# Text rows of two batches first, a table piece ahead of two slots, a later table sum, and block 0's rows by matmuls

## The reference, cut to what matters

```
h = concat([patches @ proj_w.T + proj_b + pos, txt])
xn = layernorm(layernorm(h)) * ln_w
Q = xn[:, None] * W_qk ; attn = softmax(causal(Q @ Q.T / sqrt(192)))
h = h + ((attn @ (xn - mean(wte))) / (row + 1)) @ W_o.T       # wte: 50257 x 192
n = rmsnorm(layernorm(h)) * ffn_ln_w
probs = softmax(n @ w_router) ; expert = argmax(probs)         # 16 experts
keep  = rank of the token within its expert and batch <= 64
y = relu(n @ wi[expert]) @ wo[expert]   if kept, else n
h = h + layernorm(h) + max(probs) * y
```

## Time and profile before

| | |
|---|---|
| median of 3 runs | 367.31 us (365.68 to 370.08) |
| profiled execution | 367.87 us, span 366.0 us |
| TensorE busy | 334.5 us, 91% |
| Vector, Pool, Scalar busy | 228.0, 167.7, 126.2 us |
| mean granted clock of TensorE | 0.967 |
| Vector busy from 200 to 210 us | 9.83 of 10 us |
| share of the transfer engines, 20 to 60 us | 1.01 to 1.06 |
| idle of Scalar, waiting for row maxima | 51.2 us |

### The profile page before, as it was taken

The page is one execution under the profiler, slowest core; times in us unless marked ns, Lnnn a source line. Parts: engine busy times, 40 slices in busy tenths (PEclk is TensorE's granted clock), DMA queues, the critical chain, the costliest instruction groups (busy, mean ns, idle before and its releaser), DMA issues.

```text
span 366.0 us, 6697 instructions
## 1 busy us (share of the span) xinstructions
PE 334.5 (91%) x2336; PEld 306.0 (84%) x2336; DVE 228.0 (62%) x557; ACT 126.2 (34%) x437; POOL 167.7 (46%) x180
## 2 busy tenths in 40 slices
PE   8499969899999999999998979999949999999992
PEld 3388859799899898997997969999815999999991
DVE  0669768789688787796888977657485222222221
ACT  2056543552545436534545024446610111111110
POOL 3173943755854846657548011250661134444321
PEclk9969989999999999999999978999998999999997
DMA  8899999289999995799997969400232699999940
GB/s 252 264 430 282 260 247 217 77 170 230 219 232 230 196 239 143 139 236 270 246 211 199 324 191 289 112 2 1 100 107 73 183 293 266 266 264 260 266 118 17
DMA packets 21096, 74.29 MB, mean 203 GB/s; under 512 B 3540, under 2 KB 9173, under 8 KB 20306
## 3 DMA queue, kind: packets, MB, share of 16 engines
q1 hardware_dynamic: 11362, 43.16, 38.5%
q0 software_dynamic: 6800, 27.82, 37.0%
q10 hardware_dynamic: 2912, 3.04, 3.0%
HBM read 66.12 MB, written 9.25 MB: 206 GB/s over the span
## 4 chain that ended last, share of the span: by engine, by line
PE 66%; DVE 13%; DMA 8%; ACT 5%; issue 5%; ACTq 1%; POOL 0%; POOLq 0%; DVEq 0%
PE bO L1224 18%; PE bS L1224 15%; PE bE L1224 14%; PE bJ L1224 12%; DMA wx<-in_wte 6%; ACT PB L563 2%; DMA hB<-in_txtB 2%; PE bT L1311 2%; DVE wx L856 1%; PE bT L1576 1%; DVE wbuf L856 1%; PE bT L1317 1%; PE bT L1270 1%; DVE oTA L823 1%; ACT pay L620 1%
## 5 line engine op out<-in xcount | busy, mean ns | idle before, releaser
L423 POOL TENSOR_TENSOR PA<-PA,rn 128x512 f32<-128x512 f32 x24 | 25.4, 1057 | 81.5 <-DVE rn L813 81.5
L401 POOL TENSOR_TENSOR AwA<-zT,w 96x512 f32<-96x512 f32 x45 | 50.1, 1192 | 17.4 <-ACT zT L540 17.4
L1224 PE MATMUL bJ<-wo_sb,oTA 128*128 128x192 f32 x288 | 52.7, 333 | 0.0
L558 ACT ACTIVATE PA<-bS,negmax 128x128 f32<-128x128 f32 x96 | 34.0, 367 | 51.3 <-DVE negmax L801 51.2
L1224 PEld LDWEIGHTS bS<-zT,AwA 96*128 96x128 f32 x384 | 47.3, 194 | 1.3 <-issue 0.2
L1224 PEld LDWEIGHTS bJ<-wo_sb,oTA 128*128 128x128 f32 x288 | 47.4, 194 | 0.0
L1224 PE MATMUL bS<-zT,AwA 96*128 96x128 f32 x384 | 47.1, 276 | 0.0
L1224 PE MATMUL bO<-PA,wx 96*128 96x112 f32 x384 | 45.4, 275 | 0.5 <-DVE PA L1197 0.5
L1224 PEld LDWEIGHTS bO<-PA,wx 96*128 96x128 f32 x384 | 44.9, 192 | 0.7 <-DVE PA L1197 0.7
L468 POOL DMA_INDIRECT out<-PA,yrow x16 | 15.1, 942 | 56.0 <-DVE PA L1213 56.0
L695 ACT ACTIVATE AwA<-bO 128x448 f32<-128x448 f32 x16 | 8.7, 544 | 78.5 <-PE bO L1224 52.9
(11 more groups left out here) (252 smaller groups left out, 705.5 us busy)
## 6 DMA issues: line engine op xcount, KB each, us to landing
wbuf<-in_wte POOLq DMA_DIRECT2D x10, 1344.0 KB, 12.7
wx<-in_wte POOLq DMA_DIRECT2D x8, 1344.0 KB, 12.0
wx<-in_wi SPq DMA_DIRECT2D x16, 576.0 KB
wx<-in_wo SPq DMA_DIRECT2D x16, 576.0 KB
wx<-in_wte SPq DMA_DIRECT2D x12, 672.0 KB, 9.2
dispatched<-zeros SPq DMA_DIRECT2D x7, 675.5 KB, 9.0
wbuf<-in_wte SPq DMA_DIRECT2D x2, 1344.0 KB, 7.0
wx<-in_wte SPq DMA_DIRECT2D x2, 1344.0 KB, 17.6
```

The costliest lines, as they stand in the source:

```text
L401: nc.gpsimd.tensor_tensor(o, zT[:, k, ss].unsqueeze(1).to_broadcast(list(o.shape)), w2[:, k, hs].unsqueeze(2).to_broadcast(list(o.shape)), ...
L423: nc.gpsimd.tensor_tensor(t, t, q.unsqueeze(2).to_broadcast(list(t.shape)), ALU.mult).then_inc(p_ready, 1)
L558: last = nc.scalar.activation(PA[:, h, :], bank[:, j * SA:(j + 1) * SA], ACT.Exp, bias=negmax[:, h:h + 1], accum_out=lsum[:, h:h + 1])
L1224: return nc.tensor.matmul(o, l, r, start=start, stop=stop, skip_group_check=True)
```

## The change

- Text tails and text rows of batches 0 and 1 are loaded and summed ahead of the others, on both queues; the constants come behind the small loads. The squared weights are made first on Vector. factors(1, 2, 2) stands ahead of a wait, the variances of batches 2 to 7 ahead of batch 0's first low part. The router's scaled weights are made within batch 0. One matmul of ones at the start is dropped.
- Sync loads plain piece 0 behind wo_attn, ahead of slots 2 and 3, and waits for tok_ready 5 there. Pool adds one chunk in batch 0 and three in each of batches 1 to 5; before it was 2, 3, 3, 2, 3, 3. In batch 0 Vector does plain_sum 1 behind the second maximum.
- In batch 6 TensorE does the second scores before wte_mean. On Vector a row maximum and a low part stand inside table_total, and mean_rows and mean_text come behind e_copy, row_factor and value_low. Transpositions and projections alternate anew.
- Block 0's transposed rows are made by 22 matmuls of norm with a 0/1 matrix (select, dispatch): where a token's place equals the column's number. Sync loads block 1's rows first. Scalar waits for the scatters before it loads block 3's. The rows of tokens that were not kept are made around block 0. stay_warm goes from 3, 10 and 26 to 8 and 6.

```
+        SEL0, SEL1 = 2 * EMB + 2 * T, XBUF * DW + FC * T
+        sels = ((0, 6, paf[:, SEL0:SEL0 + 6 * T].rearrange("p (j c) -> p j c", j=6)),
+                (6, SLOTS, Awf[:, SEL1:SEL1 + (SLOTS - 6) * T].rearrange("p (j c) -> p j c", j=SLOTS - 6)))
         posI, dropI = sb("posI", [128, SLOTS], i32), sb("dropI", [128, SLOTS], i32)
...
-
-            for q in range(XBUF):
+        def for_blocks(eng, step):
+
+            step(0, 0)
+            nb = count_blocks(eng)
+            for q in range(1, XBUF):
                 step(0, q)
...
-            def plain_loads(sp):
-
-                sp.wait_ge(tok_ready, 5)
-                for n in range(WPLAIN):
+            def plain_loads(sp, n0, n1):
+
...
-                sp.dma_start(H[p0:p1, 0:NBATCH, :], txtA[p0 - IMG:p1 - IMG]).then_inc(txt_in, 16)
+            for b0, b1, arrived in ((0, 2, txt_in), (2, NBATCH, txt2_in)):
+                for p0, p1 in ((IMG, 116), (116, 128)):
+                    sp.dma_start(H[p0:p1, b0:b1, :], txtA[p0 - IMG:p1 - IMG, b0:b1]).then_inc(arrived, 16)
             sp.dma_start(H[0:BP, NBATCH:SLOTS, :], txtBp).then_inc(late_in, 16)
...
             sp.wait_ge(cst_in, 16)
-            sp.wait_ge(hb_in, 16)
+            sp.wait_ge(hb2_in, 16)
             sp.wait_ge(pos_in, 32)
             sp.wait_ge(w_in, 32)
-            sp.wait_ge(txt_in, 32)
+            sp.wait_ge(txt2_in, 32)
             for s in range(2):
                 sp.dma_start(wchunk[s], wv[:, s, :]).then_inc(wte_first[s], 16)
             sp.dma_start(wo_sb[:, :, :], wo_attn).then_inc(wo_in, 16)
+            sp.wait_ge(tok_ready, 5)
+            plain_loads(sp, 0, 1)
             for s in range(2, WBUF):
                 sp.dma_start(wchunk[s], wv[:, s, :]).then_inc(wte_first[s], 16)
             sp.dma_start(cst2[:], cst2_d[:, 0:C_MAT]).then_inc(cst2_in, 16)
             sp.dma_start(wtail[:], wte[VOCAB - WTAIL:VOCAB, :]).then_inc(wtail_in, 16)
-
-            plain_loads(sp)
+            plain_loads(sp, 1, WPLAIN)
...
-            for q in range(XBUF - 1):
+            for q in (1, 0, 2):
...
                 for c in chunks[0:1]:
-                    add_wte(c)
+                    if c is not None:
+                        add_wte(c)
...
-                iteration(b, range(WBUF + 2 + 16 * b // 6, WBUF + 2 + 16 * (b + 1) // 6))
+                c = WBUF + 3 * b
+                iteration(b, range(c, c + 3) if b else (None, WBUF + 2))
...
-            act.dma_start(cst[:], cst_d).then_inc(cst_in, 16)
+            act.dma_start(hB[:, 0:2, :], txtB[:, 0:2]).then_inc(hb_in, 16)
             for dst, src in ((w2[:], wqk), (ln96[:], lnw)):
                 act.dma_start(dst, src).then_inc(w_in, 16)
             for dst, src in ((posb, pos), (pbb, projb)):
                 act.dma_start(dst, src).then_inc(pos_in, 16)
-            act.dma_start(hB[:], txtB).then_inc(hb_in, 16)
+            act.dma_start(cst[:], cst_d).then_inc(cst_in, 16)
+            act.dma_start(hB[:, 2:NBATCH, :], txtB[:, 2:NBATCH]).then_inc(hb2_in, 16)
...
-                if h == 3:
+                if h == 7:
...
-            nt_copy(0)
             exps(LAST, (1,))
             o_copy(b, 3)
+            values(LAST)
+            nt_copy(0)
             nt_copy(1)
-            values(LAST)
+            exps(LAST, (2,))
             nt_copy(2)
             nt_copy(3)
...
-                if not (is0(i) and q == 0):
+                if is0(i) and q == 0:
+                    act.wait_ge(scattered, 16 * SLOTS)
+                else:
                     act.wait_ge(y_ready, b)
...
+            def text_stats(b0, b1):
+                for b in range(b0, b1):
+                    last = nc.vector.bn_stats(st6[0:SB, 1, b, :], hB[:, b, :])
+                link(last)
+                for b in range(b0, b1):
+                    last = nc.vector.bn_aggr(mv[0:SB, 1, b, :], st6[0:SB, 1, b, :])
+                link(last)
+
+            dve.wait_ge(w_in, 16 * 2)
+            link(nc.vector.tensor_tensor(w2[:, :, :], w2[:, :, :], ln96[:, :].unsqueeze(2).to_broadcast([EC, 2, HEADS]), ALU.mult))
+            link(nc.vector.tensor_tensor(w2[:, :, :], w2[:, :, :], w2[:, :, :], ALU.mult))
+            nc.vector.tensor_scalar(w2[:, :, :], w2[:, :, :], float(EMB) ** -0.5, None, ALU.mult).then_inc(w2_ready, 1)
...
+                row_max(LAST, 0)
                 link(nc.vector.tensor_tensor(chunk_rows(w, 0, 3), chunk_rows(w, 0, 3), chunk_rows(p, 0, 3), ALU.add))
                 link(nc.vector.tensor_tensor(chunk_rows(w, 0, 3), chunk_rows(w, 0, 3), chunk_rows(w, 3, 6), ALU.add))
+                t_low(LAST - 1, 3)
                 nc.vector.tensor_tensor(chunk_rows(w, 0, 1), chunk_rows(w, 0, 1), chunk_rows(w, 1, 2), ALU.add)
                 link(nc.vector.tensor_tensor(chunk_rows(w, 2, 3), chunk_rows(w, 2, 3), chunk_rows(w, 6, 7), ALU.add))
...
+            factors(1, 2, 2)
             dve.wait_ge(t_used, 1)
             nc.vector.tensor_tensor(AwB[:, 0, :, :], zT[:, 0, SA:SEQ].unsqueeze(1).to_broadcast([EC, HEADS, SB]),
                                     w2[:, 0, :].unsqueeze(2).to_broadcast([EC, HEADS, SB]), ALU.mult).then_inc(awB0_ready, 1)
-            factors(1, 2, 2)
+            dve.wait_ge(hb2_in, 16)
+            text_stats(2, NBATCH)
...
             dve.wait_ge(t_ready, 1)
             z(1)
             row_factor(0, 2)
+            variances(2, NBATCH)
             def b_rows(b):
...
                 e_copy(b, 0)
                 t_low(b, 2)
                 e_copy(b, 1)
+                if is0(b):
+                    dve.wait_ge(late_in, 16 * 5)
+                    nc.vector.memset(oneX[:], 1.0)
+                    nc.vector.tensor_tensor(wr_sb[:, :, :], wr_sb[:, :, :], flc[:, :].unsqueeze(2).to_broadcast([EC, 2, EXP]),
+                                            ALU.mult).then_inc(wr_ready, 1)
                 e_copy(b, 2)
-                if is0(b):
-                    variances(2, NBATCH)
                 if not is0(b):
                     plain_sum(b, 0)
                 row_max(b + 1, 0)
                 if is0(b):
                     plain_sum(b, 0)
-                plain_sum(b, 1)
+                else:
+                    plain_sum(b, 1)
                 t_low(b, 3)
                 row_factor(b + 1, 0)
                 t_low(b, 4)
                 row_max(b + 1, 1)
+                if is0(b):
+                    plain_sum(b, 1)
                 plain_sum(b, 2)
...
+            def select(B):
+
+                k0, k1 = STAGE[B]
+                link(nc.vector.tensor_tensor(part(posG, B), part(drop, B), part(posF, B), ALU.add))
+                for j0, j1, sel in sels:
+                    lo, hi = max(j0, k0), min(j1, k1)
+                    if lo < hi:
+                        bc = [128, hi - lo, T]
+                        nc.vector.tensor_tensor(sel[:, lo - j0:hi - j0, :], cst2[:, C_IO:C_IO + T].unsqueeze(1).to_broadcast(bc),
+                                                posG[:, lo:hi].unsqueeze(2).to_broadcast(bc), ALU.is_equal).then_inc(sel_ready, 1)
...
             residual_b(0)
             table_total()
             residual_b(1)
-            row_max(LAST, 0)
+            row_factor(LAST, 0)
+            t_low(b, 4)
             centred_router()
             mean()
-            t_low(b, 3)
-            row_factor(LAST, 0)
-            mean_rows()
-            t_low(b, 4)
+            row_max(LAST, 1)
             dve.wait_ge(ohz_ready, 3)
-            mean_text()
-            row_max(LAST, 1)
-            row_stats(0, 4)
             e_copy(b, 3)
             row_factor(LAST, 1)
             value_low(LAST)
+            mean_rows()
+            mean_text()
+            row_stats(0, 4)
+            row_max(LAST, 2)
             row_stats(4, 8)
-            row_max(LAST, 2)
             row_factor(LAST, 2)
...
             base_factors(1)
+            select(0)
...
             place(1)
+            select(1)
...
             xt_copy(0)
+
+            dve.wait_ge(be_row, 1)
+            link(nc.vector.tensor_copy(beI[:, 0:MAXB], bS[0][0:1, 0:MAXB]))
+            link(nc.vector.tensor_scalar(beI[:, 0:MAXB], beI[:, 0:MAXB], EXP - 1, None, ALU.bitwise_and))
+
+            nc.vector.tensor_scalar(nbI[:, 0:1], cum[0:1, 1, EXP - 1:EXP], 1.0 / T, EXP + 0.25, ALU.mult, ALU.add).then_inc(tab_ready, 1)
+
+            dropped_norms()
...
+                start = is0(i) and q == 0
                 dve.wait_ge(h1_sum, b + 1)
                 nc.vector.tensor_scalar(hT[:, 4:6, :], bO[1][:, 0:2 * T].rearrange("p (c n) -> p c n", c=2), 0.0, None,
                                         ALU.max).then_inc(h1_ready, 1)
+                if start:
+                    dropped_rows(0, 5)
                 xt_copy(b + 1)
                 if q >= 2 or not is0(i):
                     dve.wait_ge(y_out[p], (i * 2 + q // 2) * 16)
...
                 nc.vector.tensor_copy(yrow[p][:, :], xb[q][:, D_ROW:D_ROW + 1])
                 dve.wait_ge(y_sum, b + 1)
```

(53 more changed lines are left out.)

77 lines of the change are left out of this document (36 added, 41 removed).

## The result

The changed kernel took **352.77 us** (median of 4 runs, 351.13 to 356.26), the kernel before beside it on the same chip 367.15 us (4 runs). The ratio is 0.961 [0.952, 0.971]. The prediction was 350, within 345 to 358. The profiled execution took 352.87 us (span 351.0, mean granted clock 0.984).

What follows compares the result with a forecast made beforehand. TensorE, busy 91% of the span, was taken as the bound except in four places; 5.9 + 3.8 - 0.2 + 4.1 + 4.0 = 17.6 us off 367.87 gave 350.3, median-adjusted 349.7, stated as 350; range 345 to 358.

Steps and rivals of the forecast that it cites:

- (a): Start: text of two batches first brings the first transposition earlier and keeps the clock up; 5.9 us gained.
- (d): Hand-off to the experts: block 0 made by matmuls, so block 1 starts 4.9 us earlier; 4.0 us gained after clock allowance.
- (c): Table's end: sum behind the second scores removes 2.67 us idle and 3.4 of slow clock; net 4.1, bounds 1.0 and 6.1.
- (b): Batch 0: first plain piece ahead of two slots removes TensorE's idleness and low clock, 5.35 us; net 3.8.
- The variances: Batch 0: six batches' variances ahead of the low part TensorE needs; 0.7 to 3.1 us lost, taken as 1.0.
- The parts add up: Whole kernel: the gains sum to 17.6 us, since each part ends in a stretch that TensorE bounds.
- the accumulated piece: Pool: one accumulated chunk leaves batch 0 and joins batch 3, for -0.2 us.
- The 0.9 for a clock that falls: Hand-off: 0.9 us taken off the gain for a clock partly low in block 0 or 1.
- Transfers that set batch 0's pace: Rival, batch 0: piece or slot lands 3 us late, Vector or Pool stands, clock falls; 354 us, chance 0.17.
- a sign of being wrong: Vector or Pool still waiting for the table in batch 0, clock falling in any of four places, or comparisons delaying the scatters.
- The table's end turning to Vector: Rival: Vector bounds the table's end, so that term gives only 1.0 us; 353 us, chance 0.12.
- The clock falling at the hand-off: Rival: blocks 0 and 1 run in low clock, block 1 loses 1.7 to 2.5 us more; 353 us, chance 0.07.

Runs made afterwards that it cites:

- (a) alone: Changed kernel with (b), (c) and (d) undone, so only the first two batches' text loaded first: 374.6 us (one run; kernel before beside it 369.17).
- (b) undone: Changed kernel with first plain piece behind all slots, Vector's old batch 0 order, third accumulated piece back in batch 0: 370.64 us, ratio 1.005.
- (a) undone: Changed kernel with all eight batches' text rows and tails in single transfers, constants first, 14 matmuls of ones at the start: 356.51 us, ratio 0.968.
- (d) undone: Changed kernel with block 0's rows coming back from memory and transposed like the others, no comparisons, 39 matmuls of ones: 357.25 us, ratio 0.969.

## Why the prediction was right, and where it was not

That the total came so near is luck: the second largest term had the wrong sign, and the errors of (a) and (d) made up for half of it.

**The step that failed is (c)**, "together 6.1 ... net 4.1". It gave -1.3. Three things were wrong in it. The projected mean came late as foreseen, but by 3.13 us, not 1.8: Vector's four low parts in front of it took 3.1 us (211.63 to 214.68) where they take 0.8 in batch 0 (45.66 to 46.41), beside Pool's normalisation and weighted rows. That was my reason for the lower bound of this term, and I had taken a value above the middle. The price stood in the trace of before: in batch 2 the same four parts take 3.1 us (82.20 to 85.25). Two short waits (0.21 and 0.30) stood where I had 0.2. So the waits went from 2.67 to 3.64 us. And the 3.4 us of slow clock, the larger half of the sum, was not tied to the wait that was removed: in another place and in two pieces, the clock was low for the same 6.8 us. At equal low clock the new order is the slower one: 47.5 against 46.2 us with 6.8 us of it, 45.9 against 45.2 with 3.4. So it costs about a microsecond by itself, and the rest is the clock. Even the execution without a spell (44.3) gained only 1.9 us on the kernel before.

**(a)**: the path was right but for its first step, which was the transfer of the text rows and not TensorE's embedding; the size was 1.4 too low at the first scores: the rows came at 10.4 instead of 10.8, the way from there to the first transposition took 3.67 us instead of 4.0, and transposition and embedding together won 2.4 us (5.31 to 2.87), where I had counted the embedding alone (1.8). At batch 0's first value step 6.2 us of the 7.3 are left (36.79 to 30.57; 6.4 in (a) alone).

**(b)**: 3.8, as forecast, if it is counted from the first scores; counted from batch 0's first value step it is 4.9 (11.1 - 6.2). The variances, for which I took 1.0 us, took 1.2 on Vector (0.50 and 0.70) with TensorE idle 0.87 in front of its next transposition; yet in (b) undone and (a) alone, which have them later, that value step comes at 30.68 and 30.36, so little of it was lost. "The parts add up" was wrong, too, and the reader should not take the agreement for proof. (b) with (a) undone is worth 5.5 us at batch 2 (92.15 - 86.62), near the 5.35 of my working; with (a) it is worth 21.2 in the two traces (102.25 - 81.02), 17.9 by the medians of all runs (370.64 - 352.77); (a) without (b) is worth -7.7. The two together give 11.1. I had asked whether the piece comes in time in the changed kernel, and said yes, rightly. I had not asked what each part would be without the other, and gave the accumulated piece -0.2 for a place worth 7.3. Slot 2 came 2.3 us after Pool wanted it, where I had 2.5 us of slack. From batch 0 to 1 the kernels with (b)'s order and the factors in their place take 24.3 us where Pool stands 0 us for slot 2, 24.7 with 0.94, 25.3 with 1.51 and 25.7 with 2.30 to 3.00, so the late slot goes with about 1.4 us. (The prediction's "batch 1's last value step about 42" is a slip: it means batch 0's, which came at 41.57.)

**(d)**: 5.2 for 4.0 in the traces, 4.5 by the medians with (d) undone. The 0.9 for a clock that falls did not come in this execution, nor did the pause of 1.5 us in front of block 1's rows. The last scatter became 1.44 us shorter, since Vector's products no longer lie beside it; from the row loads on, block 1 gained 4.5 (15.4 - 10.9), where I had 4.9; the last indices came 0.3 us late against batch 7, and 0.4 were lost behind block 1's start.

**The rivals.** Transfers that set batch 0's pace (17%) happened in part: Vector had its piece in time and the clock held, but Pool waited for the table in batch 0, which the prediction names as a sign of being wrong. Either half of (b) left out brings on the rest. The rival's "about half the rate whatever it is queued in front of" is not borne out: behind slots 2 and 3 instead of ahead of them the piece made Vector stand 10.2 us. The table's end turning to Vector (12%) is what happened, and worse than its 1.0; the clock fell there, a second of the named signs. The clock falling at the hand-off (7%) did not happen here and did in two relatives of this kernel. None of these three alone would have taken the time out of the range. The errors of +1.4 (a), -5.4 (c) and +1.2 (d), with +0.1 for the piece, leave the 2.6 or 2.7 us by which the gain was off (17.6 forecast, 15.0 between the spans). Had (a) and (d) come out at their forecast, the time would have been near 355.4, an estimate (352.8 + 2.6), still within the range.

## What to carry to other kernels

A stage made earlier is a gain only if the transfers it needs get earlier as well; where their share is full already, reorder them in the same change, or, as in (b) undone here, the stage stands and the clock is lost too. Take a slow spell of TensorE's clock that you hope to remove as a chance, not as a gain: a wait of 3.13 us cost the clock in six kernels out of seven with the same code there, and one of about 2.06 in one of three. A spell cost 1.6 us here; read the granted clock in each version, and in more than one execution where you can. Small Vector operations beside Pool's multiplications are priced by Pool's, not by their size, and which one is hit changes from execution to execution. Where parts meet at a shared resource, undo each alone before you believe that they add up.
